# Group normalisation sums by way of 32 groups, packed parameters and later border loads in a two-layer attention and expert kernel

## The chip, the cores and the metric

The kernel runs on one core of a Trainium2 chip. The metric is the device time of one execution in microseconds (us), as the median of several runs. TensorE (PE in the rows) does matmuls, VectorE (DVE) the elementwise work and the reductions, ScalarE (ACT) the activations, GpSimd (POOL) elementwise work and a part of the DMA issues, and SyncE (SP) the other DMA issues.

## The reference

The input x is (2 images, 48, 48, 384 channels) in fp32. Two residual layers follow, each behind a group normalisation with 32 groups of 12 channels (mean and variance over all pixels and the 12 channels of a group):

```
x = x + L0(gn(x))     # neighbourhood attention: 12 heads of 32, 7x7 window, 16 register keys
x = x + L1(gn(x))     # 4 experts, top 2, 384 -> 96 -> 384 each, exact gelu
```

So there are four normalisations in all: of both images ahead of the attention, and of both images ahead of the experts.

## The kernel before, in words

Channels lie on the 128 partitions (three chunks, KC = 3), pixels along the free axis. Each fp32 operand of a large product is split into an fp16 high and low half, and a product is nine fp16 matmuls: three chunks times (high, high), (high, low), (low, high) (`split_product`, L1038).

The attention goes in six stages `gi` (two images times three groups of four heads). A stage computes keys for six strips (`keys`), queries for six tiles (`queries`), and between the queries of stages 1 to 5 the output projection of the stage before (`project_out`), then the values, the scores, the maxima, and for each tile the exponentials and the weighted sums. Keys, queries and values travel through DRAM scratch arrays (`kscr`, `qscr`, `vscr`) to change their layout. The order of the work is written out by hand for each engine, and semaphores connect the engines. Every engine executes its own list in order.

A group normalisation consists of these steps, for `n` = 0 to 3:

- VectorE: `block_statistics` (L446) for the 18 pieces of an image, three `bn_aggr` and two small operations (`aggregate`, L448), which leave mean and mean square of each channel in `mv` and raise `gn_st`.
- TensorE: `group_means` (L1045) multiplies `mv` by the 384x384 matrix `G`, whose entry is 1/12 where two channels are in one group. Only neighbouring chunks share a group, so these are seven fp32 matmuls of two columns. It raises `gn_mm`.
- VectorE: `parameters` (L455) copies the sums out of PSUM and forms the variance; ScalarE takes the square root (`deviation`, L796); VectorE: `more_parameters` (L462) forms the reciprocal and the shift and raises `gn_par`.
- ScalarE and VectorE: `normalised` and `low_half` write the high and the low half of the normalised image.

For n = 0 this stands at the start of the program, behind the load of the first image. For n = 1 and 2 TensorE has `group_means` between the keys and the queries of stages 2 and 5 (L1216), and VectorE has `parameters` behind `queries_low` of tile 0 (L618). For n = 3 it lies within the expert layer, between `hidden(7)` and `hidden(8)` (L1371), and VectorE has `parameters` behind `weigh(7)` (L750).

`keys_low` (L508, DVE) for each strip writes the low half of the keys and copies both halves to `KT` (L519); from the fourth strip on that copy waits for the DMA that empties the buffer (`kw_out`). `queries(gi, 0)` and `queries(gi, 1)` wait for the third and fourth `keys_low`, and `project_out(gi - 1, 0)` waits for all six.

At the start SP issues the six parts of the first image (L232), the first weights (L233), two mask tables (L234, L236) and more weights. GpSimd issues the 24 KB of register vectors, five small parameter arrays (the last of them `rb`, which is broadcast to 128 partitions), `G`, the identity `ID16`, and, behind a memset, two zero borders of `vscr` (L316 to L325). PE keeps itself busy with 26 matmuls on zeros (L1206) as soon as a memset of GpSimd is done. ScalarE first runs one Square on `ob`, then converts the registers, the first weights (`weights_high(0)`, L810), and then takes the square root. VectorE has `weights_low(0)` (L493) ahead of `parameters(0, 7)`:

```
V.tensor_copy(cols["warm"], cols["qkb"][:, 0:1]).then_inc(s_["b16"], 1)
weights_low(0)
parameters(0, 7)
more_parameters(0)
```

## Time and profile before

| | |
|---|---|
| median of 3 runs | 680.63 us |
| lowest and highest | 676.43 and 681.11 us |
| the profiled execution | 682.01 us |
| its span | 680.2 us |
| mean granted TensorE clock | 0.967 of full speed |
| busy: PE, DVE, ACT, POOL | 591.2, 475.6, 303.2, 285.0 us |
| DMA | 95.94 MB, mean 141 GB/s |

The span runs from the first to the last instruction that the profile shows; 1.8 us of the execution's time lie around it. A busy share is a mean over stages with different limits, so it does not say what one edit is worth.
### The profile page before, as it was taken

To read this page: it belongs to the slowest core of one execution; us is meant where nothing else is said; L and a number is where in the kernel's file an instruction comes from. 1 tells how busy PE (TensorE), PEld (TensorE's weight loads), DVE (VectorE), ACT (ScalarE), POOL (GpSimd) and SP (SyncE) were. 2 spreads that over 40 slices of the span, in tenths; PEclk is the share of its full clock that TensorE was granted. 3 is DMA by queue.
4 is the path that set the end of the run, shared out by engine and by line. 5 is a ranking of instruction groups with operands and counts; after the bars stand their busy time and mean duration, and the time that the engine had idled before them with its cause. 6 is when DMAs were issued, how large, how long until landed. Compare 5 with 4: busy or idle time off the path is not lost.

```text
span 680.2 us, 22432 instructions
## 1 busy us (share of the span) xinstructions
PE 591.2 (87%) x9235; PEld 413.0 (61%) x9235; DVE 475.6 (70%) x1030; ACT 303.2 (45%) x598; POOL 285.0 (42%) x425
## 2 busy tenths in 40 slices
PE   3578778999799987998899988988878888997997
PEld 2336656677666766567675766757656454564554
DVE  4786465788787889876667868876798875772332
ACT  0663345314554277513562255441774527544231
POOL 4106588235232564436892452224646112212231
PEclk9979689999999999999999999998998998997999
DMA  8959584797419952398518954199530010110112
GB/s 296 177 128 279 168 215 123 192 238 204 118 31 232 274 152 73 84 237 235 145 51 199 250 175 136 37 248 242 164 92 22 1 36 35 56 51 35 71 44 97
DMA packets 131806, 95.94 MB, mean 141 GB/s; under 512 B 67437, under 2 KB 125481, under 8 KB 131705
## 3 DMA queue, kind: packets, MB, share of 16 engines
q1 hardware_dynamic: 121960, 75.18, 43.3%
q0 software_dynamic: 9744, 19.33, 9.1%
q8 instruction: 73, 1.20, 0.8%
q14 instruction: 29, 0.23, 0.1%
HBM read 58.11 MB, written 35.54 MB: 138 GB/s over the span
## 4 chain that ended last, share of the span: by engine, by line
PE 51%; DVE 17%; DMA 11%; SPq 9%; ACT 5%; issue 5%; POOL 2%; ACTq 0%; DVEq 0%; POOLq 0%
PE ps L1041 38%; SPq L270 6%; DVE MX L549 5%; PE ps L1200 4%; DMA KB<-kscr 4%; PE ps L1151 4%; DMA WR<-in_wqkv 2%; DMA vscr<-VT 2%; PE ps L1177 2%; DVE GT_ L481 2%; ACT XH L807 1%; SPq L253 1%; DMA VR<-vscr 1%; DVE SUMT L562 1%; DMA kscr<-KT 1%
## 5 line engine op out<-in xcount | busy, mean ns | idle before, releaser
L549 DVE TENSOR_REDUCE MX<-ps 128x2 f32<-128x456 f32 x216 | 125.4, 626 | 56.4 <-PE ps L1151 55.4
L1041 PE MATMUL ps<-XH,WQ 128*128 128x384 f16 x810 | 146.5, 337 | 9.3 <-DVE XH L491 8.0
L1041 PEld LDWEIGHTS ps<-XH,WQ 128*128 128x128 f16 x810 | 79.8, 101 | 68.2 <-issue 15.2
L866 ACT ACTIVATE PT<-ps 128x448 f32<-128x448 f32 (+1 forms) x162 | 78.7, 511 | 62.6 <-PE ps L1177 62.0
L1151 PE MATMUL ps<-KB,QS 120*32 120x228 f16 x1728 | 66.2, 270 | 29.9 <-DMA KB<-kscr 11.9
L425 POOL TENSOR_TENSOR KT<-QS,KT 128x384 f16<-128x384 f32 x36 | 32.7, 919 | 110.1 <-ACT KT L955 110.1
L1177 PE MATMUL ps<-QS,KB 122*128 122x112 f16 (+1 forms) x864 | 64.5, 215 | 10.2 <-ACT PT L866 5.6
L1041 PE MATMUL ps<-WQ,XH 128*128 128x128 f16 x972 | 63.2, 224 | 2.6 <-issue 2.1
L372 POOL DMA_DIRECT2D QS<-MT x72 | 38.2, 534 | 63.9 <-ACT MT L856 63.8
L1200 PE MATMUL ps<-PT,VR 128*32 128x112 f32 (+1 forms) x1296 | 61.1, 262 | 2.8 <-DMA VR<-vscr 2.8
L1151 PEld LDWEIGHTS ps<-KB,QS 120*32 120x32 f16 x1728 | 34.6, 97 | 47.4 <-DVE MX L549 17.4
L1041 PE MATMUL ps<-KT,WQ 128*128 128x384 f16 x324 | 59.6, 330 | 4.2 <-DVE X L710 4.1
L1177 PEld LDWEIGHTS ps<-QS,KB 122*128 122x128 f16 x864 | 43.8, 100 | 31.2 <-ACT PT L866 14.8
L1041 PEld LDWEIGHTS ps<-WQ,XH 128*128 128x128 f16 x972 | 56.7, 100 | 9.3 <-issue 6.6
L1041 PE MATMUL ps<-OS,WO 128*128 128x384 f16 x324 | 57.6, 326 | 3.1 <-DVE KT L519 1.6
L1200 PE MATMUL ps<-PT,ONE 128*32 128x112 f32 (+1 forms) x1296 | 59.8, 258 | 0.0
L703 DVE TENSOR_TENSOR QS<-ps,QS 128x384 f32<-128x384 f32 x36 | 19.8, 556 | 52.2 <-POOL KT L425 21.7
L1041 PEld LDWEIGHTS ps<-KT,WQ 128*128 128x128 f16 x324 | 31.0, 98 | 28.2 <-DVE X L710 8.0
L377 POOL TENSOR_TENSOR OS<-ON,OS 128x384 f16<-128x384 f32 x36 | 33.8, 940 | 33.9 <-ACT OS L872 33.6
L1041 PEld LDWEIGHTS ps<-OS,WO 128*128 128x128 f16 x324 | 31.0, 98 | 25.6 <-issue 3.0
L385 POOL TENSOR_SCALAR X<-X,SM 128x384 f32<-128x384 f32 x36 | 44.5, 1243 | 0.4
L948 ACT ACTIVATE QS<-ps,SM 128x384 f32<-128x384 f32 x36 | 20.7, 579 | 53.2 <-PE ps L1041 48.0
(169 smaller groups left out, 1010.0 us busy)
## 6 DMA issues: line engine op xcount, KB each, us to landing
KB<-kscr SPq DMA_DIRECT2D x108, 192.0 KB, 7.5
kscr<-KT SPq DMA_DIRECT2D x72, 192.0 KB, 2.5
VR<-vscr SPq DMA_DIRECT2D x216, 56.0 KB
QS<-qscr SPq DMA_DIRECT2D x108, 96.0 KB, 6.8
out<-X SPq DMA_DIRECT2D x12, 576.0 KB, 3.3
X<-in_x SPq DMA_DIRECT2D x6, 576.0 KB, 8.2
qscr<-QT POOLq DMA_DIRECT2D x18, 192.0 KB, 3.5
qscr<-PT POOLq DMA_DIRECT2D x18, 192.0 KB, 5.1
```

What stands on the lines that cost most here:

```text
L270: sp.dma_start(VR[0:8 * KW, s % 2, a, :], vscr[8 * a:8 * a + 8, CT_ * s:CT_ * s + KW, :]).then_inc(vr_in[s % 2][a // 3], 16)
L372: pool.dma_start(QS[SROWS + part:SROWS + part + 1, :, s * SN:(s + 1) * SN], MT[part * HEADS:(part + 1) * HEADS, s % 2, :]).then_inc(m_in[s ...
L377: nc.gpsimd.tensor_tensor(OS[:, 1, s * SN:(s + 1) * SN], ON[:, s % 2, :], OS[:, 0, s * SN:(s + 1) * SN], ALU.subtract).then_inc(s_["os_lo" ...
L385: nc.gpsimd.tensor_scalar(xs(img, c, s * SN, SN), xs(img, c, s * SN, SN), cols["obx"][:, c:c + 1], None, ALU.add).then_inc(s_["ob_add"], 1)
L425: nc.gpsimd.tensor_tensor(HW[:, m % 2, 1, k, :], HF[:, unit % 2, :], HW[:, m % 2, 0, k, :], ALU.subtract).then_inc(s_["hl"], 1)
L549: V.tensor_reduce(out=MX[:, s % 2, t, 2 * pair:2 * pair + 2], in_=ps[:, S_BANK(s, i), 0:2 * RUN].rearrange("p (h n) -> p h n", h=2), op=AL ...
L866: A(PTS[n % 4][:, 0:w], ps[:, ST_BANK(n), 0:w], ACT.Exp, scale=SCORE).then_inc(s_["exd"], 1)
L948: A(GE[:, unit % 2, :], ps[:, unit % 2, 0:SN], ACT.Gelu, bias=cols["fb1"][:, unit % KC:unit % KC + 1], scale=1 / WS).then_inc(s_["ge"], 1)
L1041: last = mm(bank, lhsT(a, k), rhs(b, k), start=(k == 0 and n == 0), stop=(finish and k == steps - 1 and n == 2))
L1151: last = mm(ps[32 * j:32 * j + 32, S_BANK(s, i), hh * RUN:(hh + 1) * RUN], QS[0:SROWS, h, q0:q0 + 32], KB[0:SROWS, h, slot(s), CHUNK * a:C ...
L1177: last = mm(ps[:, ST_BANK(n), h * w:(h + 1) * w], KB[0:TROWS, h, slot(s), LEAD + CHUNK * a:LEAD + CHUNK * (a + 1)], QS[0:TROWS, h, s * SN ...
L1200: last = mm(ps[DH * h:DH * (h + 1), bank, CT_ * q0:CT_ * q1], lhsT, PTS[n % 4][:, h * w:(h + 1) * w], start=(a == 0), stop=(a == STRIPS - ...
```

## The change

1. The matrix `G` (384x384, 576 KB) is gone. `group_sums` multiplies `mv` by `GD` (384x32) into 32 rows, three fp32 matmuls, and raises `gn_gs`; VectorE copies the 32x2 result to `GM` (`group_copy`, raises `gn_gc`); `group_means` then multiplies by `GU` (32x384), three more fp32 matmuls with 32 rows. At n = 1 and 2 `group_sums` takes the old place, `group_means` stands behind `queries(gi, 0)`, and VectorE has `group_copy` behind the last `keys_low` of the stage. At n = 3 `hidden(8)` lies between the two.
2. The register vectors and the five small parameter arrays become one array `cst` of 128x67, with `rb` repeated on the host, loaded by one DMA.
3. The DMAs of the identity and of the two zero borders wait until the last part of the first image has landed.
4. ScalarE's first activation is a Sqrt on the array of ones and no longer a Square on `ob`, so the Sqrt table is loaded at the start.
5. At the start VectorE makes the low halves of the registers and `qkb16` between the second and third chunk of the statistics, and `weights_low(0)` moves from ahead of `parameters(0, 7)` to behind the first two `normalised`.

```diff
+CONSTS = 19 + KC * REGS
...
-        G = sb("G", [P, KC, C])
+        GD = sb("GD", [P, KC, GROUPS])
+        GU = sb("GU", [GROUPS, C])
+        GM = sb("GM", [GROUPS, 2])
...
-        RR = sb("RR", [P, KC * REGS])
...
-        for name, n in (("qkb", 6), ("qkb16", 6), ("bv", 3), ("ob", 3), ("fb1", 3), ("rb", 4), ("mv", 6), ("sq", 3),
+        for name, n in (("qkb", 6), ("bv", 3), ("ob", 3), ("fb1", 3), ("rb", 4), ("regs", KC * REGS), ("qkb16", 6), ("mv", 6), ("sq", 3),
...
-            pool.dma_start(RR[:, :], regs).then_inc(s_["r_in"], 16)
-            for src, dst in ((qkb, cols["qkb"]), (bv, cols["bv"]), (ob, cols["ob"]), (fb1, cols["fb1"]), (rb.partition_broadcast(P), cols["rb"])):
-                pool.dma_start(dst, src).then_inc(s_["c_in"], 16)
-            pool.dma_start(G[:, :, :], gmat).then_inc(s_["g_in"], 16)
-            pool.dma_start(ID16[:, :], ident16).then_inc(s_["i_in"], 16)
+            pool.dma_start(SM[:, 0:CONSTS], cst).then_inc(s_["c_in"], 16)
+            pool.dma_start(GD[:, :, :], gdown).then_inc(s_["g_in"], 16)
+            pool.dma_start(GU[:, :], gup).then_inc(s_["g_in"], 16)
             nc.gpsimd.memset(ONE[:, :], 1.0).then_inc(s_["ones"], 1)
             nc.gpsimd.memset(SUMT[0:H, :], 0.0).then_inc(s_["zeros"], 1)
-            pool.wait_ge(s_["zeros"], 1)
-            for side in (0, W + 3):
-                pool.dma_start(vscr[:, side:side + 3, :], SUMT[0:H, :]).then_inc(s_["vpad"], 16)
             nc.gpsimd.memset(KU[:, :, :, :, 0:3], 0.0).then_inc(s_["pads"], 1)
             nc.gpsimd.memset(KU[:, :, :, :, W + 3:PADW], 0.0).then_inc(s_["pads"], 1)
             nc.gpsimd.memset(KB[0:96, :, :, 0:LEAD], 0.0).then_inc(s_["pads"], 1)
             nc.gpsimd.memset(KB[0:96, :, :, SLOTW - TAIL:SLOTW], 0.0).then_inc(s_["pads"], 1)
+            pool.wait_ge(x_in[0][KC - 1][1], 16)
+            pool.dma_start(ID16[:, :], ident16).then_inc(s_["i_in"], 16)
+            pool.wait_ge(s_["zeros"], 1)
+            for side in (0, W + 3):
+                pool.dma_start(vscr[:, side:side + 3, :], SUMT[0:H, :]).then_inc(s_["vpad"], 16)
...
+            def group_copy(n, bank):
+                dve.wait_ge(s_["gn_gs"], n + 1)
+                V.tensor_copy(GM[:, :], ps[0:GROUPS, bank, 0:2]).then_inc(s_["gn_gc"], 1)
+
             def parameters(n, bank):
                 dve.wait_ge(s_["gn_mm"], n + 1)
-                link(V.tensor_copy(cols["gs"], ps[:, bank, 0:2 * KC]))
+                link(V.tensor_copy(cols["gs"], ps[:, bank, 8:8 + 2 * KC]))
...
+                if c == 1:
+                    dve.wait_ge(s_["c_in"], 16)
+                    dve.wait_ge(s_["rhi"], 1)
+                    V.tensor_tensor(RG[:, 1, :, :].rearrange("p k n -> p (k n)"), cols["regs"], RG[:, 0, :, :].rearrange("p k n -> p (k n)"),
+                                    ALU.subtract).then_inc(s_["rlo"], 1)
+                    V.tensor_scalar(cols["qkb16"], cols["qkb"], WS, None, ALU.mult).then_inc(s_["b16"], 1)
             link(last)
             aggregate()
-            dve.wait_ge(s_["r_in"], 16)
-            dve.wait_ge(s_["rhi"], 1)
-            V.tensor_tensor(RG[:, 1, :, :].rearrange("p k n -> p (k n)"), RR[:, :], RG[:, 0, :, :].rearrange("p k n -> p (k n)"),
-                            ALU.subtract).then_inc(s_["rlo"], 1)
-            dve.wait_ge(s_["c_in"], 16 * 5)
-            link(V.tensor_scalar(cols["qkb16"], cols["qkb"], WS, None, ALU.mult))
-            V.tensor_copy(cols["warm"], cols["qkb"][:, 0:1]).then_inc(s_["b16"], 1)
-            weights_low(0)
+            group_copy(0, 7)
             parameters(0, 7)
             more_parameters(0)
+            dve.wait_ge(s_["b16"], 1)
...
                         for k in range(2):
                             normalised(0, a, k)
+                        if a == 0:
+                            weights_low(0)
...
+                if gi in (2, 5):
+                    group_copy(gi // KC + 1, 0)
...
             weigh(6)
+            group_copy(3, 5)
             weigh(7)
             parameters(3, 5)
...
-            act.wait_ge(s_["c_in"], 16 * 5)
-            A(cols["warm"], cols["ob"][:, 0:1], ACT.Square)
-            act.wait_ge(s_["r_in"], 16)
-            A(RG[:, 0, :, :].rearrange("p k n -> p (k n)"), RR[:, :], ACT.Copy).then_inc(s_["rhi"], 1)
+            act.wait_ge(s_["ones"], 1)
+            A(cols["warm"], ONE[:, 0:1], ACT.Sqrt)
+            act.wait_ge(s_["c_in"], 16)
+            A(RG[:, 0, :, :].rearrange("p k n -> p (k n)"), cols["regs"], ACT.Copy).then_inc(s_["rhi"], 1)
             weights_high(0)
             deviation(0)
...
+            def group_sums(n, bank):
+                pe.wait_ge(s_["gn_st"], n + 1)
+                for k in range(KC):
+                    last = mm(ps[0:GROUPS, bank, 0:2], GD[:, k, :], mv[:, k, :], start=(k == 0), stop=(k == KC - 1))
+                last.then_inc(s_["gn_gs"], 1)
+
             def group_means(n, bank):
-                pe.wait_ge(s_["gn_st"], n + 1)
+                pe.wait_ge(s_["gn_gc"], n + 1)
                 for j in range(KC):
-                    near = [k for k in range(KC) if abs(k - j) < 2]
-                    for k in near:
-                        last = mm(ps[:, bank, 2 * j:2 * j + 2], G[:, k, j * P:(j + 1) * P], mv[:, k, :], start=(k == near[0]), stop=(k == near[-1]))
+                    last = mm(ps[:, bank, 8 + 2 * j:10 + 2 * j], GU[:, j * P:(j + 1) * P], GM[:, :], start=True, stop=True)
                 last.then_inc(s_["gn_mm"], 1)
...
-            pe.wait_ge(s_["g_in"], 16)
+            pe.wait_ge(s_["g_in"], 32)
+            group_sums(0, 7)
             group_means(0, 7)
...
-                    group_means(gi // KC + 1, 0)
+                    group_sums(gi // KC + 1, 0)
                 for s in range(TILES):
                     queries(gi, s)
+                    if gi in (2, 5) and s == 0:
+                        group_means(gi // KC + 1, 0)
...
+            group_sums(3, 5)
+            hidden(8)
             group_means(3, 5)
-            hidden(8)
             result(1)
...
+    member = (group[:, None] == np.arange(GROUPS)[None, :]).astype(np.float32)
+    consts = [column(qkv_b[:2 * C]), column(qkv_b[2 * C:]), column(L0_conv_out_b), column(np.asarray(L1_conv_fc1_b).reshape(-1)),
+              np.broadcast_to(np.asarray(L1_conv_router_b).reshape(1, -1), (P, EXPERTS)), flat(np.asarray(L0_conv_registers).T)]
```

TensorE around the queries of stage 2, before. `ps<-XH,WQ` are the keys (above) and the queries (below) of `split_product`, `ps<-SM,G` the group means, `ps<-OS,WO` the output projection.

```order
L1041 MATMUL ps<-XH,WQ 128x384 x8
L1050 MATMUL ps<-SM,G 128x2 [waits t_ev,gn_st,mx,kr_lo]
L1050 MATMUL ps<-SM,G 128x2 x6
L1041 MATMUL ps<-XH,WQ 128x384 [waits k_lo]
L1041 MATMUL ps<-XH,WQ 128x384 x8
L1041 MATMUL ps<-XH,WQ 128x384 [waits k_lo]
L1041 MATMUL ps<-XH,WQ 128x384 x8
L1041 MATMUL ps<-OS,WO 128x384 [waits os_lo,wolo,k_lo]
L1041 MATMUL ps<-OS,WO 128x384 x8
```

The same place in the changed kernel (its line 1052 is the old 1041).

```order
L1052 MATMUL ps<-XH,WQ 128x384 x8
L1059 MATMUL ps<-SM,GD 32x2 [waits t_ev,gn_st,mx,kr_lo]
L1059 MATMUL ps<-SM,GD 32x2 x2
L1052 MATMUL ps<-XH,WQ 128x384 [waits k_lo]
L1052 MATMUL ps<-XH,WQ 128x384 x8
L1065 MATMUL ps<-GM,GU 128x2 [waits gn_gc]
L1065 MATMUL ps<-GM,GU 128x2 x2
L1052 MATMUL ps<-XH,WQ 128x384 [waits k_lo]
L1052 MATMUL ps<-XH,WQ 128x384 x8
L1052 MATMUL ps<-OS,WO 128x384 [waits os_lo,wolo,k_lo]
```

The seven matmuls ahead of the first queries became three there and three between the first and the second queries, with a new wait for `gn_gc`.

VectorE in the same stage, before: the last strips of `keys_low` (`KU` and `KT`), then `queries_low` (`QT`) and `parameters` (`SM`).

```order
L511 SCALAR_TENSOR_TENSOR KU<-ps,SM,KU 128x8x48 [waits k_hi]
L519 COPY KT<-KU 128x6x112 [waits kw_out2,chain]
L519 COPY KT<-KU 128x6x112
L525 SCALAR_TENSOR_TENSOR QT<-ps,SM,QT 128x384 [waits q_hi]
L457 COPY SM<-ps 128x6 [waits gn_mm]
```

And in the changed kernel.

```order
L517 SCALAR_TENSOR_TENSOR KU<-ps,SM,KU 128x8x48 [waits k_hi]
L525 COPY KT<-KU 128x6x112 [waits kw_out2,chain]
L525 COPY KT<-KU 128x6x112
L459 COPY GM<-ps 32x2 [waits gn_gs]
L531 SCALAR_TENSOR_TENSOR QT<-ps,SM,QT 128x384 [waits q_hi]
L463 COPY SM<-ps 128x6 [waits gn_mm]
```

The new copy, which raises `gn_gc`, stands behind both copies of the last strip. Stage 5 has the same order on both engines.

VectorE at the start, from the aggregation on, before.

```order
L450 BN_AGGR SM<-ST 128x2 x2
L452 TENSOR_TENSOR SM<-SM 128x3 [waits chain]
L453 TENSOR_TENSOR SM<-SM 128x3 [waits chain]
L580 TENSOR_TENSOR RG<-RR,RG 128x48 [waits rhi,r_in]
L583 TENSOR_SCALAR SM<-SM 128x6 [waits c_in]
L584 COPY SM<-SM 128x1 [waits chain]
L495 SCALAR_TENSOR_TENSOR WQ<-WR,WQ 128x1152 [waits whi]
L457 COPY SM<-ps 128x6 [waits gn_mm]
```

And in the changed kernel.

```order
L452 BN_AGGR SM<-ST 128x2 x2
L454 TENSOR_TENSOR SM<-SM 128x3 [waits chain]
L455 TENSOR_TENSOR SM<-SM 128x3 [waits chain]
L459 COPY GM<-ps 32x2 [waits gn_gs]
L463 COPY SM<-ps 128x6 [waits gn_mm]
L464 TENSOR_TENSOR SM<-SM 128x3 [waits chain]
L465 SCALAR_TENSOR_TENSOR SM<-SM 128x3 [waits chain]
L470 RECIPROCAL SM<-SM 128x3 [waits gn_sd]
L471 SCALAR_TENSOR_TENSOR SM<-SM 128x3 [waits chain]
L487 TENSOR_SCALAR GT_<-X,SM 128x384 [waits b16,gn_par]
L487 TENSOR_SCALAR GT_<-X,SM 128x384
L501 SCALAR_TENSOR_TENSOR WQ<-WR,WQ 128x1152 [waits whi]
```

The operation that waits for the converted weights (`whi`) moved from ahead of the parameters to behind the first two normalised blocks.

## Rows read from the trace of the kernel before

**Rows 1.** The page: busy time, share of the span and instructions of each engine.
```profile
PE 591.2 (87%) x9235; PEld 413.0 (61%) x9235; DVE 475.6 (70%) x1030; ACT 303.2 (45%) x598; POOL 285.0 (42%) x425
```
**Rows 2.** The chain that ended last, 0 to 46 us: start us, us, what.
```profile
4.20 15.97 DMA WR<-in_wqkv
20.19 1.17 ACT WQ L812
21.38 1.36 DVE WQ L495
```
**Rows 3.** The timeline, 0 to 28 us: start, length, engine, line, operation, tiles, count [idle before].
```profile
16.40 1.48 DVE L446 BATCH_NORM_STATS2 ST<-X 128x6 f32<-128x384 f32 x3 [0.25 <-DMA X<-in_x]
...
19.12 3.12 PE L1050 MATMUL ps<-SM,G 128*128 128x2 f32 x14 [5.08 <-DVE SM L453]
...
21.37 1.28 ACT L798 ACT_TABLE_LOAD   x1
...
22.66 0.15 DVE L457 COPY SM<-ps 128x6 f32<-128x6 f32 x1
...
23.24 0.20 ACT L798 ACTIVATE SM<-SM 128x3 f32<-128x3 f32 x1 [0.59 <-DVE SM L459]
...
23.89 0.87 DVE L481 TENSOR_SCALAR GT_<-X,SM 128x384 f32<-128x384 f32 x2
...
27.13 5.20 PE L1041 MATMUL ps<-XH,WQ 128*128 128x384 f16 x18 [2.87 <-DVE XH L491]
```
**Rows 4.** Windows of the loading phase: busy time by engine, then clock, DMA share, GB/s.
```profile
8.30:10.20 1.90, 1.38 (x8) 1.24 (x9) 1.46 (x3) 0.00 (x0) 1.06 (x2) 1.00 0.87 106
10.20:16.40 6.20, 3.85 (x20) 3.06 (x18) 2.96 (x6) 0.34 (x2) 0.00 (x0) 1.00 1.03 402
```
**Rows 5.** DMA issues, 0 to 70 us: KB each, us from issue to landing.
```profile
G<-in_gmat POOLq DMA_DIRECT2D x1, 576.0 KB, 9.7
...
vscr<-SUMT POOLq DMA_DIRECT2D x2, 72.0 KB, 8.5
...
ID<-in_ident POOLq DMA_DIRECT2D x1, 32.0 KB, 9.6
...
SM<-in_rb POOLq DMA_DIRECT2D x1, 2.0 KB, 7.3
```
**Rows 6.** The timeline around the second group means, 203 to 210 us.
```profile
208.39 0.58 DVE L519 COPY KT<-KU 128x672 f16<-128x672 f16 x2 [0.33 <-DMA kscr<-KT]
```
**Rows 7.** The chain that ended last, 196 to 225 us.
```profile
205.23 1.46 PE ps L1050 x14
206.68 17.68 PE ps L1041 x108
```
**Rows 8.** The timeline around the third group means, 440 to 447 us.
```profile
443.63 1.64 PE L1041 MATMUL ps<-XH,WQ 128*128 128x384 f16 x9 [0.43 <-DVE KT L519]
...
445.91 0.58 DVE L519 COPY KT<-KU 128x672 f16<-128x672 f16 x2
...
446.55 1.64 PE L1041 MATMUL ps<-OS,WO 128*128 128x384 f16 x9 [1.28 <-DVE KT L519]
```
**Rows 9.** The chain that ended last, 436 to 500 us.
```profile
446.55 14.80 PE ps L1041 x90
```
**Rows 10.** The chain that ended last, 545 to 600 us.
```profile
558.67 1.46 PE ps L1050 x14
...
562.25 1.28 ACT L798
...
566.82 2.58 PE ps L1041 x9
```
**Rows 11.** Windows around two waits of TensorE: busy by engine, clock, DMA, GB/s.
```profile
440.00:446.50 6.50, 4.83 (x34) 3.15 (x32) 4.77 (x15) 3.41 (x6) 0.00 (x0) 1.00 1.03 232
...
616.00:619.70 3.70, 0.14 (x2) 0.05 (x2) 1.58 (x3) 1.94 (x5) 1.77 (x2) 0.84 0.00 0
619.70:625.40 5.70, 5.70 (x19) 2.60 (x20) 1.12 (x2) 1.02 (x2) 0.94 (x2) 0.50 0.00 0
```

More of the change, by code:

```diff
@@ L46, in slot, with build @@
     return s % 4
-def build(nc, x, wqkv, wo, fc1, fc2, rw, regs, qkb, bv, ob, fb1, fb2, rb, qtab, ktab, gmat, ident16, tri, pick, out):
+def build(nc, x, wqkv, wo, fc1, fc2, rw, cst, fb2, qtab, ktab, gdown, gup, ident16, tri, pick, out):
     ctx = ExitStack()
@@ L93, in build @@
             at += n
-        assert at <= 64
+        assert at <= CONSTS + 40
         mv = cols["mv"].rearrange("p (c s) -> p c s", s=2)
@@ L171, in dve_lows @@
             return n * GN_STEPS + blk * KC - pool_lows(n, blk)
-        names = """r_in c_in g_in i_in wo_in t_in whi wlo wohi wolo rhi rlo b16 zeros vpad bvhi bvlo bv_mm obx pads ones kr_mm kr_hi kr_lo vr_mm vr_sb krg
-            gn_st gn_mm gn_var gn_sd gn_par gn_hi gn_t gn_ta gn_lo_p gn_lo_v ob_add
+        names = """c_in g_in i_in wo_in t_in whi wlo wohi wolo rhi rlo b16 zeros vpad bvhi bvlo bv_mm obx pads ones kr_mm kr_hi kr_lo vr_mm vr_sb krg
+            gn_st gn_gs gn_gc gn_mm gn_var gn_sd gn_par gn_hi gn_t gn_ta gn_lo_p gn_lo_v ob_add
             k_mm k_hi k_lo q_mm q_hi q_lo v_mm v_sb o_mm op_done s_mm mx mxh t_mm t_ev st_mm exd pv sumt rinv norm os_hi os_lo
@@ L1458 @@
     group = np.arange(C) // (C // GROUPS)
-    gmat = (group[:, None] == group[None, :]).astype(np.float32) / np.float32(C // GROUPS)
+    member = (group[:, None] == np.arange(GROUPS)[None, :]).astype(np.float32)
+    consts = [column(qkv_b[:2 * C]), column(qkv_b[2 * C:]), column(L0_conv_out_b), column(np.asarray(L1_conv_fc1_b).reshape(-1)),
+              np.broadcast_to(np.asarray(L1_conv_router_b).reshape(1, -1), (P, EXPERTS)), flat(np.asarray(L0_conv_registers).T)]
     tri = np.broadcast_to(np.tril(np.ones((EXPERTS, EXPERTS), np.float32), -1).reshape(1, -1), (P, EXPERTS ** 2))
@@ L1470 @@
         "fc2": flat(np.asarray(L1_conv_fc2_w).transpose(0, 2, 1).reshape(EXPERTS * HID, C)),
-        "rw": flat(np.asarray(L1_conv_router_w).T), "regs": flat(np.asarray(L0_conv_registers).T),
-        "qkb": column(qkv_b[:2 * C]), "bv": column(qkv_b[2 * C:]), "ob": column(L0_conv_out_b),
-        "fb1": column(np.asarray(L1_conv_fc1_b).reshape(-1)), "fb2": np.ascontiguousarray(L1_conv_fc2_b),
-        "rb": np.ascontiguousarray(L1_conv_router_b), "qtab": query_table(), "ktab": key_tables(),
-        "gmat": rows(gmat), "ident16": np.eye(P, dtype=np.float16),
+        "rw": flat(np.asarray(L1_conv_router_w).T),
+        "cst": np.ascontiguousarray(np.concatenate(consts, axis=1)), "fb2": np.ascontiguousarray(L1_conv_fc2_b), "qtab": query_table(), "ktab": key_tables(),
+        "gdown": rows(member / np.float32(C // GROUPS)), "gup": np.ascontiguousarray(member.T), "ident16": np.eye(P, dtype=np.float16),
         "tri": np.ascontiguousarray(tri), "pick": pick,
```

2 lines of the change are left out of this document (1 added, 1 removed).

## The prediction

> **What bounds the kernel now.** I read the page first: TensorE is busy 591.2 of 680.2 us, the others much less [rows 1]. That is a mean and prices none of the edits, so I went to the chain of waits at the five places that the diff touches: the start, the second and third group means (stages 2 and 5), the fourth in the expert layer, and the DMA queue of GpSimd. The reader should look in each for what ends last.
>
> At the start it is a transfer: the first weights land at 20.2 us, ScalarE converts them, VectorE makes their low half until 22.74 [rows 2], and only then, at 22.66 in the overlapping record, copies the group means [rows 3], though TensorE was done with them at 22.24 (19.12 + 3.12). The first normalised block starts at 23.89, the keys at 27.13 [rows 3]. The statistics are not far behind: the last part of the image allows the last three pieces at 16.40.
>
> In stage 2 TensorE sets the end by itself: 1.46 us of group means, then 17.68 us without a break [rows 7]. In stage 5 it does not: it waits twice for VectorE's `KT` copies (0.43 and 1.28 us), and the run of 90 matmuls starts only at 446.55, released by the last copy [rows 8, 9]. In the expert layer the 1.46 us stand on the chain again [rows 10].
>
> **The change part by part**, against the profiled execution (682.01 us, span 680.2 and 1.8 around it; 1.4 above the median of 680.63).
>
> *Loads at the start.* G (576 KB), two borders (72 KB each) and the identity (32 KB) leave the time before the image has landed [rows 5]: 752 KB, 0.77 MB, at the 402 GB/s of 10.2 to 16.4 us [rows 4] is 1.9 us. From 8.3 to 10.2 us the DMA moves only 106 GB/s [rows 4]; at 402 these 1.9 us would have taken 0.5, so the hole costs 1.4. In it fall the small arrays; `rb`, broadcast from 16 bytes, is a 2 KB transfer that needs 7.3 us [rows 5]. I take it that the hole goes with them. The new arrays (34, 48 and 48 KB) cost 0.3. So the last part of the image comes 3.0 earlier, at 13.4, and the statistics end at 14.9. VectorE doesn't hold this up: a part is three pieces, 1.48 us [rows 3], and a part of 576 KB takes as long to arrive (0.59 MB at 402 GB/s, 1.47); the two moved operations (0.4 in all, an estimate from the 0.15 of the copy in rows 3 with room for waits) fall into the wait ahead of the fifth part. If the hole stays, the gain is 1.6.
>
> *The parameters at the start.* From the last piece's end (17.88) to TensorE's start (19.12) are 1.24 us, so the sums start at 16.15. One pass costs 3.12 / 14 = 0.22 us there [rows 3]. Six passes are 1.3, VectorE's copy with its two waits 0.4, six more passes 1.3: 19.2. From the copy of the means (22.66) to the first normalised block (23.89) are 1.2 us, and with one wait it is 20.5, 3.4 earlier. ScalarE must be free by 19.8 for its square root: the weights, shifted with the image and delayed 0.4 by identity and borders (0.18 MB), land at 17.6, and 1.17 of conversion ends at 18.8. That cover is one microsecond deep; if the weights land later than 18.6, they set the time again.
>
> The low half of the weights (1.36) now stands between VectorE's normalised blocks (0.87) and the low halves of the image. So the last low half comes at 20.5 + 0.87 + 1.36 + 1.7 (three at 0.56) = 24.4, and the first keys at 24.5, 2.6 before 27.13. TensorE's register products (1.5 us behind the weights at 22.7) end at 24.3, beside it. What follows is the same ring of keys, ScalarE and VectorE and keeps the distance. **Minus 2.6**, bounds minus 4.0 (a pass at 1.46 / 14 = 0.10 as in rows 7) and minus 1.0 (weights as late as now).
>
> *The table load.* ScalarE's load of 1.28 us at 21.37 ran while VectorE was in the low weights, and the square root itself waited 0.59 for VectorE [rows 3]. Taking it out gives nothing beyond the above. The Trainium skill ("ScalarE: Activation LUTs", What ACT_TABLE_LOAD costs) puts a switch at 1.28 us and a drain of 1.38. By that the square root could not have started before 24.0, and a switch removed would be worth 0.8 more. The row has it at 23.24, with no room for the drain, so the trace disagrees and I keep nothing.
>
> *Stage 2.* `group_copy` stands behind VectorE's last `KT` copy, which ends at 208.97 (208.39 + 0.58) [rows 6] for a reason of its own (the DMA that empties the buffer). The copy (0.15, as L457) and one handover (0.14, from VectorE's last operation to 19.12 at the start) put `gn_gc` at 209.2 for TensorE. There the three sums start at 205.23, 0.6 us (six passes at 0.10), and queries(0), 1.47, end at 207.3. Behind the wait stand the means (0.6) and queries(1), then all projections and queries of the stage. Queries(1) end at 209.2 + 0.6 + 1.47 = 211.3; now at 206.68 + 2 x 1.47 = 209.6 (1.47 is 17.68 / 12, nine matmuls [rows 7]). **Plus 1.7.** On VectorE `queries_low(0)` moves by 0.15, nobody waits for it. Bounds: 0, if a later transfer has that much to spare, and 1.9.
>
> *Stage 5.* The last `KT` copy ends at 446.49 [rows 8], the means are done at 447.3, and queries(1), 1.47, end at 448.8. Today queries(1) run from 443.63 in a time in which TensorE has to wait anyway, and the projection starts at 446.55. **Plus 2.3**, bounds 0 and 2.5. The 1.46 us of G saved there fall into the old wait and give nothing.
>
> *Clock behind stage 5.* From 440.7 to 446.7 TensorE would be busy for queries(0) alone, 1.5 of 6 us; today it is 4.83 of 6.5 at the upper level (2.4 GHz) [rows 11]. The nearest row is 616.0 to 619.7, where it was busy 0.14 of 3.7, and the following 5.7 us ran at 0.50, the lower level (1.2 GHz) [rows 11]. Nine matmuls of 384 columns took 2.58 in such a stretch and 1.47 to 1.64 otherwise [rows 7, 8, 10]. A stretch of 3.4 us at half speed loses 1.7. **Plus 1.7**, bounds 0 and 2.85 (5.7 / 2). For the 2.0 us of idleness in stage 2 I count nothing.
>
> *Expert layer.* Three sums (0.6) instead of 1.46 ahead of `hidden(8)` bring the GELU of unit 8 forward by 0.8; the chain goes from it through the table load and the square root [rows 10]. The parameters must be ready by then: means at 559.3 + 1.5 + 0.6 = 561.4, variance at 562.2, table loaded at 562.7. That cover is 0.5 deep. **Minus 0.8**, bounds minus 1.4 and 0.
>
> Sum: -2.6 + 1.7 + 2.3 + 1.7 - 0.8 = **+2.3**, 684.3 for an execution like the profiled one and 682.9 for the median.
>
> **The rivals.**
>
> *The waits cost nothing.* If a DMA behind the query stages sets the end, both waits and the clock vanish: -2.6 - 0.8 = -3.4, 677.2. For it: in stage 5 TensorE already waits. Against: the runs of 17.68 and 14.80 us on the chain [rows 7, 9] leave no gap, and all queries and values, which feed the transfers, stand behind the wait.
>
> *The start doesn't get faster as meant.* The transfers that leave the image's time return right behind it, into the time of the weights, and ScalarE has to convert these ahead of the square root. If they still land at 20.2, the first block starts at 20.2 + 1.17 + 0.7 = 22.0 and the keys at 26.1, -1.0 only: +3.9, 684.5. For it: the weights land 3.8 us behind the last part of the image. Against: they stand behind it in the same queue, so they should move with it.
>
> *Slower: the clock falls behind both new waits.* TensorE idles 2.0 us in stage 2 and 3.6 in stage 5, and both are followed by work in which it is alone on the chain. With 2.85 us lost at each, and the start at -1.0: -1.0 + 1.7 + 2.3 + 5.7 = +8.7, 689.3. It decides where the idleness of stage 2 is enough to lower the clock. For it: the fall behind 616.0. Against: the waits in 440.0 to 446.5, 1.7 us together, left the level at 1.00 [rows 11]. The Trainium skill ("TensorE: Matmul & The Clock Gate", HAM oscillation) tells of a kernel whose waits for DMA lower the clock each time, so that every burst begins cold. By it the place in stage 5 is the candidate; the trace agrees with the rule at 616 us.
>
> **How the numbers follow.** Forecast 0.50; waits for nothing 0.20; the start short 0.18; the slower one 0.07; 0.05 for more gain than any, the start at its bound of -4.0 with the waits at 0 and the expert layer at -1.4, 675.2. The time is the forecast's, 682.9. All terms at their unfavourable ends (-1.0 + 1.9 + 2.5 + 2.85) are +6.3, 686.9; three runs of one kernel already lie 4.7 us apart. So the range is 677.0 to 687.5. A measurement tells about 1% (6.8 us) from no change: faster 0.04, same 0.90, slower 0.06, the last nearly all from the clock case.
>
> **What would show it right or wrong.** In the changed profile: the last statistics should start near 13.4 and not 16.4; the window from 8.3 to 10.2 should move about 400 GB/s; the first normalised block should come at 20.5, the first keys at 24.5. In stage 2 and 5 the first matmul of the means should show idle time before it, released by VectorE (the copy into `GM`), about 2.0 and 3.6 us, and the window behind stage 5 a clock under 1.00. The prediction is wrong if the means follow queries(0) without idle time, if the start of the scores of stages 2 and 5 keeps its distance to the keys, or if the weights land at 20 us as before.

## The result and the profile after

The changed kernel takes 672.1 us (median of 11 runs, 666.3 to 675.1) where the kernel before takes 679.8 in the same session (11 runs): ratio 0.9896, 95% interval 0.9866 to 0.9927. It is faster by 1%, and outside the range of 677.0 to 687.5. Two more sessions gave 0.9895 (0.9854 to 0.9935) and 0.9876 (0.9835 to 0.9917). Weighted by their intervals the three make 0.9891 +- 0.0021, or -7.4 us of 678. The profiled execution took 672.79 us (span 671.0).

The page and the chain that ended last at the start, of the kernel after (start us, us, what):

```profile
PE 585.5 (87%) x9227; PEld 408.7 (61%) x9227; DVE 474.6 (71%) x1033; ACT 301.7 (45%) x597; POOL 281.9 (42%) x421
```
```profile
1.66 6.76 DMA X<-in_x
...
11.50 2.77 DVE ST L448 x6
...
16.19 1.45 PE ps L1065 x6
...
19.69 1.36 DVE WQ L501
```

The weights' transfer of [rows 2] is gone from the chain. VectorE's statistics set the end now: six pieces in one run with no wait ahead of them, where [rows 3] had three pieces at 16.40 released by the image. The timeline of after at the start (start, length, engine, line, operation, count, idle before):

```profile
14.95 1.16 ACT L823 ACTIVATE WQ<-WR 128x1152 f16<-128x1152 f32 x1 [8.01 <-DMA WR<-in_wqkv]
...
15.50 0.45 PE L1059 MATMUL ps<-SM,GD 128*32 128x2 f32 x6 [5.53 <-DVE SM L455]
15.99 0.15 DVE L459 COPY GM<-ps 32x2 f32<-32x2 f32 x1 [0.63 <-PE ps L1059]
...
16.19 1.44 PE L1065 MATMUL ps<-GM,GU 32*128 32x2 f32 x6 [0.24 <-DVE GM L459]
...
18.90 0.87 DVE L487 TENSOR_SCALAR GT_<-X,SM 128x384 f32<-128x384 f32 x2
19.69 1.35 DVE L501 SCALAR_TENSOR_TENSOR WQ<-WR,WQ 128x1152 f16<-128x1152 f32 x1
...
22.59 2.92 PE L1052 MATMUL ps<-XH,WQ 128*128 128x384 f16 x9
```

The first normalised block starts at 18.90 and not 23.89, the first keys at 22.59 and not 27.13 [rows 3]: 4.5 us, where the sum had 2.6. The windows (busy by engine, clock, DMA share, GB/s) and the DMA issues (KB each, us to landing) of after:

```profile
8.30:10.20 1.90, 1.67 (x9) 1.14 (x7) 1.75 (x4) 0.00 (x0) 0.00 (x0) 1.00 1.01 405
```
```profile
WR<-in_wqkv SPq DMA_DIRECT2D x1, 576.0 KB, 10.9
...
SM<-in_cst POOLq DMA_DIRECT2D x1, 33.5 KB, 5.4
ID<-in_ident POOLq DMA_DIRECT2D x1, 32.0 KB, 11.1
```

The hole of [rows 4] is closed, 405 GB/s for 106.

In stage 2 the matmuls of the second step (`group_means`) wait, as forecast, and what follows is slow: nine matmuls of 384 columns take 2.62 and 2.37 us for 1.64. Timeline, then the windows of after:

```profile
198.07 0.82 PE L1065 MATMUL ps<-GM,GU 32*128 32x2 f32 x6 [2.13 <-DVE GM L459]
198.83 2.62 PE L1052 MATMUL ps<-XH,WQ 128*128 128x384 f16 x9
201.24 2.37 PE L1052 MATMUL ps<-OS,WO 128*128 128x384 f16 x9
```
```profile
199.30:202.80 3.50, 3.50 (x14) 1.67 (x12) 0.86 (x3) 1.29 (x2) 0.31 (x1) 0.51 0.82 201
```

So it is in stage 5, where the copy into `GM` stands behind the last `KT` copy (the two views again):

```profile
437.27 0.58 DVE L525 COPY KT<-KU 128x672 f16<-128x672 f16 x2 [0.79 <-DMA kscr<-KT]
437.77 0.14 DVE L459 COPY GM<-ps 32x2 f32<-32x2 f32 x1
...
437.96 1.20 PE L1065 MATMUL ps<-GM,GU 32*128 32x2 f32 x6 [3.85 <-DVE GM L459]
...
439.09 3.06 PE L1052 MATMUL ps<-XH,WQ 128*128 128x384 f16 x9
```
```profile
438.30:445.10 6.80, 6.80 (x24) 3.62 (x24) 2.29 (x8) 2.87 (x4) 1.50 (x2) 0.50 0.85 208
```

The waits are 2.13 and 3.85 us (forecast 2.0 and 3.6), and the clock fell to its lower level behind both. Yet the kernel is 7 us faster. The experiments had to find why the waits aren't paid, and where a start of 2.6 us becomes more.

### The profile page after: what moved, and what is told of

It is laid out like the page before. It is cut to its first block, busy times and chain, and to the rows that moved or that the text cites. A ratio compares the mean times of both kernels' runs of the same rounds, so it can differ in the third digit from the quotient of the medians.

```text
span 671.0 us, 22415 instructions
## 1 busy us (share of the span) xinstructions
PE 585.5 (87%) x9227; PEld 408.7 (61%) x9227; DVE 474.6 (71%) x1033; ACT 301.7 (45%) x597; POOL 281.9 (42%) x421
## 4 chain that ended last, share of the span: by engine, by line
PE 54%; DVE 19%; DMA 8%; SPq 7%; issue 5%; ACT 4%; POOL 2%; ACTq 0%; DVEq 0%; POOLq 0%
PE ps L1052 39%; PE ps L1215 5%; PE ps L1166 5%; SPq L272 4%; DVE MX L555 4%; DMA KB<-kscr 3%; PE ps L1192 2%; DVE ST L448 2%; DMA vscr<-VT 2%; DVE GT_ L487 2%; DVE SUMT L568 1%; DMA kscr<-KT 1%; SPq L255 1%; DVE KT L525 1%; DVE RINV L574 1%
## 5 line engine op out<-in xcount | busy, mean ns | idle before, releaser
L1052 PE MATMUL ps<-WQ,XH 128*128 128x128 f16 x972 | 61.2, 220 | 4.3 <-issue 4.0
L1052 PEld LDWEIGHTS ps<-WQ,XH 128*128 128x128 f16 x972 | 55.0, 98 | 10.8 <-issue 8.0
L1052 PE MATMUL ps<-OS,WO 128*128 128x384 f16 x324 | 59.8, 334 | 1.8 <-DVE X L539 1.4
L351 POOL DMA_DIRECT2D qscr<-QT x18 | 13.3, 741 | 78.1 <-DVE QT L531 78.0
L549 DVE SCALAR_TENSOR_TENSOR X<-ps,X 128x384 f32<-128x384 f32 x90 | 44.1, 547 | 0.7 <-PE ps L1052 0.6
```

The source lines that it names most:

```text
L549: V.scalar_tensor_tensor(out=xj, in0=ps[:, OP_BANK(gi, s, j), 0:SN], scalar=1 / WS, in1=xj, op0=ALU.mult, op1=ALU.add).then_inc(s_["op_don ...
L1052: last = mm(bank, lhsT(a, k), rhs(b, k), start=(k == 0 and n == 0), stop=(finish and k == steps - 1 and n == 2))
```

## The experiments

Sixteen runs in four sessions, each kernel timed beside the kernel before. The intervals are 95%; 0.001 is 0.68 us.

| run | ratio to before | interval |
|---|---|---|
| e1, e15 two-step sums of n = 1, 2, 3 alone | 0.9999, 1.0000 | 0.9969-1.0029, 0.9969-1.0031 |
| e2, e6 start alone, `G` loaded in stage 1 | 0.9932, 0.9935 | 0.9901-0.9962, 0.9905-0.9966 |
| e14 start alone, `G` loaded at 20 us | 0.9918 | 0.9879-0.9957 |
| e13 changed, `G` loaded in stage 1 too | 0.9955 | 0.9919-0.9991 |
| e4 `rb` repeated on the host alone | 0.9988 | 0.9954-1.0023 |
| e12 late borders alone | 0.9986 | 0.9955-1.0017 |
| e5, e9 changed kernel again | 0.9895, 0.9876 | 0.9854-0.9935, 0.9835-0.9917 |
| e8 changed, early borders | 0.9941 | 0.9907-0.9976 |
| e10 changed, copies later | 0.9893 | 0.9852-0.9934 |
| e3, e11 changed, copies earlier | 0.9877, 0.9827 | 0.9835-0.9919, 0.9776-0.9877 |
| e7, e16 the same and low weights first | 0.9859, 0.9888 | 0.9805-0.9914, 0.9828-0.9948 |

**The waits alone (e1, e15).** The kernel before with two-step sums in stages 2 and 5 and in the expert layer; the start stays as it was, `GD` and `GU` are loaded late. e15 is the same kernel.

```diff
-                    group_means(gi // KC + 1, 0)
+                    group_sums(gi // KC + 1, 0)
                 for s in range(TILES):
                     queries(gi, s)
+                    if gi in (2, 5) and s == 0:
+                        group_spread(gi // KC + 1, 0)
```

> The kernel before with its start untouched; the group sums go in two steps at the second, third and fourth normalisation alone, placed as in the changed kernel. Theory W (the new wait of TensorE for VectorE's late copy costs time, and the clock falls behind it): plus 1.7 in stage 2, plus 2.3 in stage 5, plus 1.7 to 6 for the clock, minus 0.8 in the expert layer, so 5 to 9 us slower than before (0.7 to 1.3%). Rival A (the waits are absorbed by later transfers): 0 to 1 us faster than before.

> The two-step sums of stages 2 and 5 and of the last normalisation alone, as in e1, with the start of the kernel before. From the rows: +2.6 us in stage 2, +1.7 us net in stage 5, -1.3 us behind it, +3 in all; e1 gave 0 (from -2.1 to +2.0 us). Theory L expects 0 to 1.5 us, as the difference of the changed kernel and the corrected start; a value of -2 or below would say that the two-step sums give something that no row explains.

Both give no change, 0.0 +- 1.5 us together. The theory that this kernel is 5 to 9 us slower falls. That the waits as such cost nothing isn't shown by it, since both runs hold the gain of the expert layer too (below). These two profiles also show the old start again, earlier than in [rows 3]. The timeline of e1:

```profile
18.16 1.16 ACT L826 ACTIVATE WQ<-WR 128x1152 f16<-128x1152 f32 x1 [6.77 <-DMA WR<-in_wqkv]
...
26.01 2.40 PE L1055 MATMUL ps<-XH,WQ 128*128 128x384 f16 x7 [3.21 <-DVE XH L502]
```

The weights land at 18.16 here, 18.80 in e15, 20.19 in the profile of before; the keys start at 26.01, 26.42 and 27.13. The execution that the forecast was made from had a start about 1 us later than its like. From the keys' start the change is worth 3.4 to 3.8 us against these two.

**The start alone (e2, e6).** The changed kernel with the one-step sum by `G` for n = 1 to 3; `G` is loaded by POOL in stage 1.

```diff
             for gi in range(STAGES):
                 register_keys(gi)
+                if gi == 1:
+                    pool.dma_start(G[:, :, :], gmat).then_inc(s_["gg_in"], 16)
...
-                    group_sums(gi // KC + 1, 0)
+                    whole_means(gi // KC + 1, 0)
```

> The changed kernel with the one-step sums by the large matrix kept at the second to fourth normalisation (that matrix is loaded in stage 1, when the DMA is idle); the start is that of the changed kernel. Theory W: faster than the changed kernel by what the waits cost, 5 to 9 us, so 12 to 16 us faster than before. Rival A: like the changed kernel, 7 to 9 us faster than before.

> The start alone (two-step sums for the first normalisation only, one-step sums by the large matrix in stages 2 and 5) once more, beside the changed kernel. Theory A: 671 to 673, within 1 us of e5. Theory W: 3 us faster than e5. In the profile no wait of the second group-sum matmul in stages 2 and 5 and no low clock at those places.

e2 and e6 together: -4.5 +- 1.5 us. The start gives more than 2.6, but the start and the waits' 0 don't make the -7.4 of the whole. The difference of 2.9 us is larger than chance would easily give. It was put to the test below (e13, e14).

**One part of the start at a time (e4, e12).** e4 repeats `rb` on the host and nothing else; e12 moves the identity and the borders behind the image and nothing else.

```diff
-(rb.partition_broadcast(P), cols["rb"])
+(rb, cols["rb"])
```

> The kernel before with one edit: the router's bias is repeated on the host and loaded as 128 rows of 16 bytes instead of a broadcast of one row. If the broadcast is what stalls the DMA engines from 8.3 to 10.2 us, the window moves about 400 GB/s, the last part of the image and the first weights come 1.0 to 1.5 us earlier and the kernel is 1 to 1.5 us faster. If the small transfers as such make the hole, nothing changes.

> The kernel before with nothing changed but the place of two loads: identity and zero borders behind the image. e8 was 3 us slower than e5 in the total, of which the profile showed 0.7 us at the first keys. If the late borders are worth 0.5 to 0.7 us, this is within 1 us of before, and first keys at 25.5 to 26.5. If they are worth 3 us in themselves, this is 3 us faster than before. The hole at 8.3 to 10.2 us stays at about 110 GB/s, since the routing bias is still broadcast by the transfer.

The window of the hole in e4, then in e12:

```profile
8.30:10.20 1.90, 1.40 (x8) 1.24 (x9) 1.48 (x3) 0.00 (x0) 1.05 (x2) 1.00 0.99 280
```
```profile
8.30:10.20 1.90, 1.90 (x12) 1.67 (x11) 1.41 (x3) 0.00 (x0) 0.00 (x0) 1.00 0.88 105
```

The broadcast is most of the hole: without it 280 GB/s move, with it 105 (110 in e1). The rest goes with the other small arrays (405 in after). Each edit alone is worth about 1 us by its ratio, with an interval of 2.1 to 2.4 us on either side, so neither can be told from nothing. In e12 the weights landed at 19.85 although borders and identity were out of their way. A likely reason that one edit shows so little is that it is lost again at the next thing that ends last: in before those were weights, table load and sums of 3.12 us together. No run takes these out one by one.

**Borders early again (e8)**, in the changed kernel.

```diff
-            pool.wait_ge(x_in[0][KC - 1][1], 16)
...
```

> The changed kernel with the identity and the zero borders loaded at the start again, beside the image, as in the kernel before. If the late load was worth what its bytes take (216 KB at 400 GB/s, 0.5 us), image and weights land 0.5 us later and the first keys start 0.5 us later, the total 0.5 us slower, below what can be told. Rival (the late load is the larger part of the 5 us that the start gained): weights land at 17 us or later, first keys at 25, total 2 to 3 us slower than e5. Rival (the image isn't waited for any more, VectorE's statistics are): nothing moves.

Weights at 16.01 and keys at 23.26, 0.7 to 0.8 later than in e5; the ratio is 3.1 us worse than e5's, with 3.6 us of uncertainty on the difference. The rows bear out the small value, the total can't decide.

**The matrix's load (e13, e14).** e13 is the changed kernel with the 576 KB of `G` loaded in stage 1 and not used in any product (`GM` and `GU` lie in other partitions, as in e1, e2 and e14, to make room); e14 is e2 with that load moved behind the borders.

```diff
+                if gi == 1:
+                    pool.dma_start(G[:, :, :], gmat).then_inc(s_["gg_in"], 16)
```

> The changed kernel with the 576 KB of the large matrix loaded in stage 1 as in e2 and e6, and not used. Theory L (that load costs time where transfers bound stage 1, so that e2 and e6 understate the start): 1.5 to 3 us slower than the changed kernel, a ratio to before of 0.992 to 0.994. 576 KB take 1.4 us at the 410 GB/s that the hole of the start moved, or 3.2 us at the 180 GB/s that the steps of stage 1 move. Theory O (it hides): 0.989.

> The start alone, with the large matrix loaded behind the borders at about 21 us instead of in stage 1. Theory L: 1.5 to 3 us faster than e2 and e6, a ratio of 0.989 to 0.991, so that the start alone gives what the changed kernel gives, and the waits of stages 2 and 5 cost about what the shorter expert layer saves. Theory O: 0.9935 as before.

e13 loses 4.4 +- 2.8 us against the changed kernel. `G` is issued at 115.78 and lands 4.8 us later. The `KT` copy of the fourth strip of stage 1, the first that can wait, stands beside it, in e13 and in after:

```profile
122.01 0.58 DVE L528 COPY KT<-KU 128x672 f16<-128x672 f16 x2 [3.89 <-DMA kscr<-KT]
```
```profile
115.91 0.58 DVE L525 COPY KT<-KU 128x672 f16<-128x672 f16 x2 [0.24 <-DMA kscr<-KT]
```

VectorE waits 3.89 us for the transfer that empties the buffer; in e2 and e6 it waits 2.96 and 3.33, and in no profile without that load more than 1.72 at this copy. But the profiles don't show that the load costs this time: over the last three copies of the stage e13, e2 and e6 wait 4.43, 3.48 and 3.85 us, and e1, e3, e4, e5, e8 and e10, which have no such load, 3.44 to 4.25, most of it at another copy. So the cost of the load rests on the total of e13 alone. Freed of the load (e14) the start alone is -5.6 +- 2.6 us, only 1.1 +- 3.0 better than e2 and e6; that these understated the start is likely and not shown. With 0 for the two-step sums -5.6 is within the intervals of -7.4. The parts close as far as these runs can tell, no further.

**The dose of the waits (e9, e10, e11, e3, e5).** e5 and e9 are the changed kernel. In e3 and e11 `group_copy` stands behind the fourth `keys_low`, in e10 behind the first `queries_low`.

```diff
                         keys_low(gi, a)
+                        if gi in (2, 5) and a == 3:
+                            group_copy(gi // KC + 1, 0)
-                if gi in (2, 5):
-                    group_copy(gi // KC + 1, 0)
```

> The changed kernel with VectorE's copy of the 32 sums moved in stages 2 and 5 from behind the sixth to behind the fourth strip of low keys. Theory W: TensorE's idle time ahead of the second step falls from 2.1 and 3.9 us to under 0.7 us, and the kernel gains 4 to 8 us on the changed one, so 12 to 16 us faster than before. Rival A: no change against the changed kernel (7 to 9 us faster than before).

> The changed kernel once more, in the same session as the three below, so that they can be compared with it and not only with the kernel before. Theory A (the start alone gives the gain; the waits of stages 2 and 5 cost under 1 us in the total): as the start alone (e6) within 1 us, both 5 to 7 us faster than before. Theory W (the waits cost what the stage rows show, 2.6 + 1.7 us, less 1.3 us in the expert layer): 3 us slower than e6. Theory B (the two-step sums give something of their own besides the start, as 672.1 against e2's 672.0 and e1's 678.3 cannot tell): faster than e6 by 1 to 2 us. In the profile: first normalised group at 18.9, first keys at 22.6, nine slow matmuls behind the second group-sum matmul of stages 2 and 5.

> The changed kernel as the one that the three below are held against, in one session. 670 to 673; second group-sum matmul waited for 0.8 us (stage 2) and 1.2 us (stage 5), with low clock behind both waits.

> A larger dose of the wait: in stages 2 and 5 the copy of group sums stands one instruction of VectorE later, behind the low half of the first query tile, which itself waits for that tile's matmuls. The wait of the second group-sum matmul becomes about 2.5 to 4 us in both stages. Theory W (a wait of TensorE there is paid in full in the total): 4 to 6 us slower than e9. Theory A (most of it is given back, since the stages' heads behind it wait for VectorE and for transfers and not for TensorE): under 2 us slower than e9; in the profile the step from the first to the last maximum of the next stage gets shorter by about what the wait added.

> e3 once more beside the changed kernel: the copies of group sums behind the fourth low keys of stages 2 and 5. The step between the last maximum of one stage and the first of the next was 3.8 us (stage 2) and 5.4 us (stage 5) shorter in e3 than in the changed kernel, of which the steps behind gave back 1.5 and 3 to 4 us. Theory W: 3 to 4 us faster than e9. Theory A: 0 to 2 us faster.

The 0.8 and 1.2 us that e9's expectation calls waits are the lengths of the six passes in after; the waits are 2.13 and 3.85 us there, 1.81 and 3.93 in e9. e10's wait in stage 5 grew less than meant, and the total went 1.2 us up from e9's, with 3.9 on the difference:

```profile
441.32 1.44 PE L1065 MATMUL ps<-GM,GU 32*128 32x2 f32 x6 [4.37 <-DVE GM L459]
```

As a dose it is too small to decide. e3 and e11 together are at 0.9857 +- 0.0032, 2.3 us better than the changed kernel with 2.6 on the difference. The totals decide neither for the waits in full nor for nothing. The chain that ended last shows what happens in stage 5 of e9 (with the wait), and of e11 (without):

```profile
437.98 0.58 DVE KT L525 x2
438.67 1.14 PE ps L1065 x6
439.81 17.60 PE ps L1052 x99
457.41 0.70 PE ps L1166 x24
...
469.17 0.50 ACT WR L861
```
```profile
437.56 0.59 DVE KT L525 x2
438.19 14.80 PE ps L1052 x90
452.99 0.70 PE ps L1166 x24
...
458.01 2.55 issue
460.56 0.57 PE ps L1166 x15
461.13 2.63 PE ps L1052 x27
...
469.16 0.50 ACT WR L861
```

e11 comes to the scores at 452.99, 4.4 us ahead of e9, and reaches the same ScalarE instruction at 469.16 against 469.17. That the two agree to 0.01 us is chance, one profile of each. In between TensorE pauses 2.55 us and waits for nothing that the chain names ("issue"), and then the clock is at its lower level for 3.4 us (window of e11):

```profile
461.50:464.90 3.40, 3.40 (x48) 3.00 (x46) 1.24 (x4) 0.49 (x1) 0.32 (x1) 0.50 0.89 266
```

The kernel before has that pause too. Its timeline and window:

```profile
468.48 1.30 PE L1151 MATMUL ps<-KB,QS 120*32 120x228 f16 x21 [2.29 <-issue]
```
```profile
468.40:471.80 3.40, 3.32 (x41) 2.93 (x41) 1.71 (x3) 0.00 (x0) 0.00 (x0) 0.50 1.09 301
```

Of the ten profiles without the late copy eight have 0.88 to 2.82 us of such a pause there (e2 and e7 0.33 and 0.38); of the eight with it, seven have none and e15 has 1.10. So the wait for the group sums stands in front of a pause and takes its place; it takes the place of a fall of the clock in only five of the ten (before, e3, e11, e12, e16).

The pause isn't a wait for the operands `KB` and `QS`: it stands after 3 to 9 matmuls, in the middle of a product whose semaphores are all awaited ahead of its first matmul, in e2, e7 and e14 even in a product of the values, which reads neither. The page of before (and of after) lists a queue that loads instructions:

```profile
q8 instruction: 73, 1.20, 0.8%
```

These are 73 transfers of 16 KB in the whole span (1.20 MB). In each of the eleven profiles with the pause one of them stands 2.45 to 2.75 us ahead of the pause's end: at 465.85 in before (end 468.48), at 458.05 in e11 (end 460.56), at 461.30 in e14 (end 463.98). So TensorE most likely waits there for its next instructions, with the DMA engines busy (share 1.07 during the pause in before and in e11). In e9 such a transfer stands at 456.65, 0.7 us ahead of the first scores of the stage, in e11 5.1 us behind them; TensorE comes to the place in question 5.1 us behind them too, so in e9 nothing pauses. What sets when it is issued isn't shown, and no run moves it.

In stage 2 another wait stands behind. e12 has no group wait there, and its timeline shows

```profile
206.28 1.64 PE L1042 MATMUL ps<-OS,WO 128*128 128x384 f16 x9 [2.26 <-DVE KT L520]
```

So in e2, e4, e6, e12 and e14 TensorE waits 1.77 to 2.26 us for the last `KT` copy, one query tile later than the changed kernel waits 2.13 for the copy into `GM`. Only the profile of before, alone among the six kernels with one-step sums, has no such wait. The changed kernel's fall of the clock is not in its place: it stands behind the group wait in seven of the eight profiles with the late copy, and behind the wait for `KT` in one of five (e6).

All 18 profiles together put a size on it. From the first matmul of stage 2's group sums to the end of the last maximum of the attention the eight with the late copy take 304.9 us in the mean, the six with one-step sums 301.5, the four with the early copy 301.5. The late copy costs 3.4 +- 1.7 us against one step. With half of each stretch at clock 0.50 taken out, as an estimate of what the lower level costs, the difference is 0.3 +- 1.3. So against the kernel before the waits themselves cost nothing that can be told, and the two falls of the clock cost about 3. The shorter expert layer gives 2.5 +- 1.3 back, which is why e1 and e15 show 0.

**The low half of the weights first (e7, e16).** e3 with `weights_low(0)` ahead of `parameters(0, 7)`.

```diff
             group_copy(0, 7)
+            weights_low(0)
             parameters(0, 7)
```

> The changed kernel with the copies of group sums behind the fourth low keys of stages 2 and 5 (as in e3), and with the low halves of the first weights written before the normalisation's parameters, as in the kernel before, instead of behind them. VectorE waits for the group means from about 16.3 to 17.5 us, and the low halves take 1.35 us of it: if they fit into that wait, the first normalised group stays at 18.9 and the first keys start at 21.2 instead of 22.6, 1.4 us earlier, and the total is 1.4 us below e3's ratio. Rival: the halves delay the copy out of the group means by up to 0.3 us, and the first keys wait for the normalised low halves anyway: 0.5 to 1.0 us earlier. Rival: the low halves aren't what the keys wait for; then nothing changes.

> e7 once more: early copies and the low halves of the first weights ahead of the parameters. e7 gave 0.9859, e3 and e11 0.9877 and 0.9827; in the profiles the first maximum of e7 stands at 56.1 us against 55.6 to 55.9 in e3 and e11. If the order of the low halves is worth nothing, the ratio is 0.985 +- 0.004, within that of e3 and e11; if the earlier first keys (22.1 against 22.6) were worth more, it is below 0.983.

The timeline of e7:

```profile
16.39 1.36 DVE L501 SCALAR_TENSOR_TENSOR WQ<-WR,WQ 128x1152 f16<-128x1152 f32 x1 [0.31 <-ACT WQ L822]
...
22.13 4.79 PE L1051 MATMUL ps<-XH,WQ 128*128 128x384 f16 x18 [2.86 <-DVE XH L497]
```

The low half fits into VectorE's wait, but the first keys come only 0.5 us earlier. The two runs make 0.9872 +- 0.0040, within e3's and e11's: the order is worth nothing that can be told. All four runs with early copies make 0.9863 +- 0.0025, -9.3 us against before; they are the fastest tried. Against the changed kernel this is 1.9 us better with 2.2 on the difference; e7 and e11 come out below the changed kernel of their session, e3 and e16 had none beside them.

## Why the prediction was wrong

*The start: right in kind, mis-sized.* "Minus 2.6" measured 4.5 in the profile of after against that of before, 3.4 to 3.8 against e1 and e15, and 4.5 +- 1.5 (e2, e6) and 5.6 +- 2.6 (e14) in the total. Three steps were short.
- Loads: -3.0 was nearly right. POOL's wait for the image's last part ends at 12.95 in after, 3.45 before 16.40. What wasn't seen is that the statistics are then no longer held up by the image at all: they end at 14.27 (11.50 + 2.77).
- "One pass costs 0.22" for both steps. The rows of after have six passes with 32-column weights in 0.45 us, and six with 128 columns in 1.44. The first step was priced by the wrong shape, 0.85 too dear.
- "The weights land at 17.6." They landed at 14.95. The forecast kept the distance of 3.8 us between image and weights, though 576 KB at 402 GB/s need 1.5. The distance is 2.0 in after. In before the DMA moved 0.57 MB in those 3.8 us (149 GB/s). Why it is slow there isn't shown, and it isn't the rule for this start: from GpSimd's wait for the last part to the weights are 2.3 us in e1 and 2.5 in e15 (15.91 and 16.33 to 18.16 and 18.80), 3.6 in e12. This step also gave the start short its 0.18: that rival fell.

*Stage 2, "plus 1.7", and stage 5, "plus 2.3" with the clock's "plus 1.7".* Place, size and releaser of the waits were as forecast, and so was the fall of the clock behind stage 5; the rival's second fall behind stage 2 came as well. What failed is the step from a wait to the total, which took the waits' 1.7 + 2.3 = 4.0 us whole. The profiles put them at 0.3 +- 1.3 and the clock at about 3 where the sum had 1.7, together 3.4 for 5.7. The argument against the rival "the waits cost nothing" was that 17.68 and 14.80 us on the chain [rows 7, 9] leave no gap. It read one run of one line and not what follows it: the pause of 2.29 us ahead of 468.48, 7 us behind the end of [rows 9], stood in the profile of before. In stage 2 the row read was that of an exception; five other profiles wait there anyway. The rival had half of the mechanism: a transfer ends last behind the waits (of `KT`'s scratch array in stage 2, in stage 5 most likely of instructions), but the clock doesn't vanish with them. With -5.6 in place of -2.6 it gives about 674. Of the slower rival, its +8.7 leaves out the expert layer's -0.8; the sum is +7.9.

*Expert layer, "minus 0.8".* From the last maximum of the attention to the end of the span the six profiles with one-step sums take 174.3 us in the mean, the twelve with two steps 171.8. Counting half of each stretch at clock 0.50 out of both leaves 167.1 and 166.3, which is the 0.8. The other 1.7 lie in the clock, a term that the forecast put at nothing; why less time is at the lower level there isn't shown. The cover was there: the square root follows its table load at once in after as in before.

*Table load.* Nothing of its own could be seen, as forecast: in after the root waits 2.14 us for VectorE. No run tries it alone. That nothing follows the load of 1.28 us is seen better than in [rows 3] in the expert layer of before: load at 562.25, root at 563.54. The 3.12 us of G, the load and the weights seem to have hidden one another in before; that they had to go together isn't shown.

*The range.* Each term was bounded from one profiled execution. That execution had no wait at the place in stage 2 where five of six have one, which pointed to a slower forecast. It also had the latest weights of the three with this start, which made the gain look larger and worked against the miss. And from the first keys to stage 2's sums it took 177.9 us, after 171.4, though the instructions there are the same: 6.5 of the 9.2 us between the two profiles. The same distance is 176.9 and 171.2 in e3 and e11, which are one kernel. So the difference of two profiles prices nothing here.

The terms as measured make about -4 (start -4.5 to -5.6, waits and clock +3.4, expert layer -2.5, that is -3.6 to -4.7) against +2.3 forecast and -7.4 +- 1.4 in the total. The rest of about 3 us is within the uncertainty of the terms and has no cause named. The outcome belongs to the branch "more gain than any" (0.05, 675.2) and went further than it, by the sizes above and by no mechanism that was named for it.

## What to carry to other kernels

A wait found in one stage is a cost only if the next thing that ends last has no idle time of its own; look one wait further than the run that stands on the chain, and count the fall of the clock behind a wait by itself, since it can stay where the wait is absorbed. At the start of a kernel, edits that each show about 1 us can be worth 5 together. One profile can differ from the next of the same kernel by more than the effect looked for, so count over many. And when an experiment adds a transfer to put a part back, test the transfer by itself: here the changed kernel with 576 KB more in stage 1 was 4.4 +- 2.8 us slower.
